# Coupling cycles spread over the turn, features a turn ahead, and attention scores moved into the head of the turn

## The reference

```
x = _layernorm(x + _L0_attn_ref(x, ...))     # random features: exp(x.w - |x|^2/2), times a matrix
x = _layernorm(x + _L0_xattn_ref(x, ctx...)) # 16-head attention over 120 keys
x = _layernorm(x + _L0_ffn_ref(x, ...))      # "coupling": 3 cycles of a 4-layer net and a twist
x = _layernorm(x + _L1_attn_ref(x, ...))     # Mamba-like: conv, silu, softplus, 16-state scan
x = _layernorm(x + _L1_xattn_ref(x, ctx...)) # gelu(x @ ctx.T) * (x @ ctx.T) @ ctx
x = _layernorm(x + _L1_ffn_ref(x, ...))      # router, best of 8 experts, times its gate
```

## Time and profile before

| | |
|---|---|
| median of 3 runs | 3458.91 us (3455.02 to 3460.43) |
| profiled execution, its own time | 3453.69 us |
| its span, first to last instruction | 3451.9 us |
| PE / DVE / ACT / POOL busy | 77% / 75% / 46% / 44% of the span |
| TensorE clock granted, mean | 0.805 of full speed |
| HBM traffic | 13 GB/s over the span |

### The profile page before, as it was taken

How to read it: one execution, slowest core, us unless ns; L and a number is a source line. 1 busy time by engine, 2 the same in 40 slices (tenths; PEclk the granted TensorE clock), 3 DMA queues, 4 the chain that set the end, 5 groups by cost and what they waited for, 6 DMA issues and landing times.

```text
span 3451.9 us, 41745 instructions
## 1 busy us (share of the span) xinstructions
PE 2672.9 (77%) x10956; PEld 1520.7 (44%) x10956; DVE 2598.4 (75%) x4316; ACT 1571.6 (46%) x2870; POOL 1505.1 (44%) x1159
## 2 busy tenths in 40 slices
PE   5877878787787878878787787887778787787746
PEld 3435435354453535445354453544445354443413
DVE  2387786968779696877868778687887968778693
ACT  1363545535455443544545444443544544454440
POOL 0064461725427172561725427163461726436180
PEclk8868778887887888788887887878878887888777
DMA  3000000000000000000000000000000000000000
GB/s 116 8 8 0 21 1 28 0 22 6 0 28 0 27 0 21 7 0 27 0 22 6 0 28 0 27 0 7 21 0 27 0 22 6 0 12 0 12 0 12
DMA packets 16786, 45.63 MB, mean 13 GB/s; under 512 B 2376, under 2 KB 6992, under 8 KB 16336
## 3 DMA queue, kind: packets, MB, share of 16 engines
q1 hardware_dynamic: 16592, 43.90, 3.5%
HBM read 35.50 MB, written 8.39 MB: 13 GB/s over the span
## 4 chain that ended last, share of the span: by engine, by line
PE 48%; DVE 25%; issue 12%; ACT 9%; POOL 3%; DVEq 1%; ACTq 0%; DMA 0%; SPq 0%; POOLq 0%
PE bank L487 46%; DVE h_ring L1014 9%; POOL ysum L1534 3%; DVE x L392 3%; DVE x L1111 2%; DVE smax L919 2%; ACT a_ring L1379 2%; PE bank L400 2%; DVE ln_stats L374 2%; DVE xpad L1020 1%; ACT bank L1374 1%; ACT spare L1319 1%; DVE qT L969 1%; DVE x L1091 1%; DVE x12T L971 1%
## 5 line engine op out<-in xcount | busy, mean ns | idle before, releaser
L1534 POOL TENSOR_TENSOR ysum<-ysum,h_ring 128x512 f32<-128x512 f32 x896 | 1152.3, 1286 | 490.8 <-DVE h_ring L1014 428.1
L1014 DVE TENSOR_TENSOR_SCAN h_ring<-a_ring,bank 128x512 f32<-128x512 f32 x1024 | 1170.6, 1198 | 103.8 <-ACT a_ring L1379 51.3
L487 PE MATMUL bank<-w_expert_w,x45T 128*128 128x512 f32 x1024 | 621.5, 746 | 197.8 <-DVE x L1111 196.2
L1379 ACT ACTIVATE a_ring<-soft,decay 128x510 f32<-128x510 f32 x1024 | 660.2, 712 | 119.7 <-DVE h_ring L1014 118.2
L487 PEld LDWEIGHTS bank<-w_expert_w,x45T 128*128 128x128 f32 x1024 | 221.7, 235 | 485.1 <-DVE x L1111 247.7
L1515 POOL TENSOR_TENSOR x<-x,w_rows 128x1024 f32<-128x1024 f32 x16 | 47.9, 2992 | 851.7 <-PE bank L400 851.7
L1289 ACT ACTIVATE spare<-bank 120x512 f32<-120x512 f32 x256 | 138.1, 591 | 449.5 <-PE bank L487 449.5
L487 PE MATMUL bank<-spare,w_cn_w 128*128 128x256 f32 (+2 forms) x768 | 278.4, 472 | 44.0 <-ACT spare L1323 20.3
L400 PE MATMUL bank<-w_ident,x 128*128 128x128 f32 x640 | 135.7, 347 | 223.4 <-DVE x L392 223.4
L1111 DVE SCALAR_TENSOR_TENSOR x<-bank,weight,x 128x256 f32<-128x256 f32 x512 | 212.3, 471 | 72.2 <-PE bank L487 72.2
L966 DVE TENSOR_SCALAR couple<-gate,gate_scale,base 128x256 f32<-128x256 f32 x96 | 40.0, 416 | 275.9 <-ACT gate L1333 275.9
(11 more groups left out here) (144 smaller groups left out, 3836.5 us busy)
## 6 DMA issues: line engine op xcount, KB each, us to landing
x0T<-in_xT SPq DMA_DIRECT2D x16, 512.0 KB, 3.3
x<-in_x SPq DMA_DIRECT2D x16, 512.0 KB, 4.2
out<-x SPq DMA_DIRECT2D x16, 512.0 KB, 3.2
ctxT<-in_ctxT SPq DMA_DIRECT2D x16, 240.0 KB, 4.3
ctxTb<-in_ctxT SPq DMA_DIRECT2D x16, 240.0 KB, 2.6
ctxb<-in_ctx SPq DMA_DIRECT2D x16, 240.0 KB, 3.0
w_expert_w<-in_expert_w SPq DMA_DIRECT2D x1, 2048.0 KB
w_winT<-in_winT SPq DMA_DIRECT2D x1, 1024.0 KB
```

The costliest lines, as they stand in the source:

```text
L487: return pe.matmul(o, l, r, start=start, stop=stop)
L1014: scanned.then(v.tensor_tensor_scan(h_ring[:, k % HRING, :], a_ring[:, k % RING, :, :].rearrange("p b s -> p (b s)"), xc2, 0.0, ALU.mult, ...
L1379: a.activation(a_ring[:, k % RING, :, 1:S], delta[:, c, :].rearrange("p (b s) -> p b s", b=NB)[:, :, 1:S], ACT.Exp, scale=decay[:, k:k + 1 ...
L1534: p.tensor_tensor(out=total, in0=first, in1=h_ring[:, k % HRING, :], op=ALU.add)\
```

## The change

Three groups' work is still done in each turn, but a fourth, nxt = f+1, is served in part:

- **Coupling.** The six steps are three cycles of two (`cycle(f, 0)`, `cycle(f, NB)`, `cycle(f, 2 * NB)`), apart from each other by decays on ACT, experts on PE and scans on DVE. Each has its own load of the GELU table and of the log/exp table behind it: 9 loads in a turn and not 5. The matmuls `mamba_out` no longer stand between the layers; they open the next turn, with the layernorm of that group behind them.
- **Features ahead.** The random features, keys, values, first projection and first layernorm of nxt are done in the second half of the turn, so x, xT and ctxT are loaded apart and earlier.
- **Scores into the head.** All 16 score steps and their maxima stand ahead of the first scan, between the parts of `mamba_in` and `convolve`, on three banks and not four.
- RING is 12 (8 before); softplus goes chunk by chunk; the squares of chunks 1 to 3 are made at decays 20, 34 and 48 (before: at the fifth decay of the chunk, 20, 36 and 52); a copy of m's x is kept for its layernorm (`keep`, 1024 elements on ACT).
- The loop has 13 turns; turn 15 stands behind it without an nxt.

The diff, cut to its core. In the three `turn` functions the guards (`if f is not None:` and the like) are left out, and what they guard keeps its indent; lines that were removed there are not shown.

```diff
-RING = 8
+RING = 12
 HRING = 6
 OUT_AFTER = 4
-SQUARE_AT = 4
+SQUARE_AT = (0, 20, 34, 48)
...
-        SCORES = [bank[0], bank[1], bank[2], bank[5]]
-        OUT12 = [bank[2], bank[0]]
+        OUT1 = [bank[2], bank[4]]
+        OUT2 = [bank[2], bank[0]]
+        QUERY = [bank[2], bank[0]]
+        TURN1 = [bank[0], bank[1]]
+        IN = [bank[4 + j % 2][:, :] for j in range(2 * IC)]
...
-                    if u >= 4:
-                        pe.wait_ge(smax_ready.sem, smax_ready.at(g, u - 2))
+                    if u >= 2:
+                        pe.wait_ge(smax_ready.sem, smax_ready.at(g, u - 1))
                     for e in range(DC):
                         for r in (r0, r0 + 1):
-                            last = mm(SCORES[r][:, e * 240:(e + 1) * 240],
+                            last = mm(bank[(u + r - r0) % 3][:, e * 240:(e + 1) * 240],
                                       qT[r * 32:(r + 1) * 32, e, t * P:(t + 1) * P],
...
+            def cycle(f, s):
+                for n in range(1, 5):
+                    for k in (s, s + 1):
+                        if n > 1 or s >= NB:
+                            layer(f, n, k)
+                        if n == 2 and k == 0:
+                            glob(f, 3)
+            def turn(f, m, b, nxt):
                     rotate_back(m, 1)
+                    mamba_out(b, 0, 12)
+                    norm_turn(pe, n1, f, TURN1)
+                    norm_turn(pe, n3, m, TURN)
+                    mamba_out(b, 12, 16)
+                    queries(f)
+                    mamba_in(m, 0, 2)
+                    scores(f, 0, 2)
+                    mamba_in(m, 2, IC)
                     norm_turn(pe, n4, b, MB)
+                    scores(f, 2, 4)
                     gated_in(b)
+                    mamba_in(m, IC, IC + 2)
+                    scores(f, 4, 6)
+                    mamba_in(m, IC + 2, 2 * IC)
+                    scores(f, 6, 8)
+                    turn_maxima(f, m)
+                    gated_out(b)
+                for k in range(SLOTS + 2):
                         attend(f, k, k + 1)
+                        if k == 3:
+                            norm_turn(pe, n5, b, MB)
+                        elif k == 5:
+                            router(b)
+                        elif k == 9:
+                            turn_weights(b)
+                        elif k == 11:
+                            expert_bias(b)
+                        elif k in (13, 15):
+                            experts(b, (k - 13) // 2, (k - 11) // 2)
+                    rfs(nxt, 0, f)
+                    experts(b, 2, 3)
+                    project(f, n2, ctxnT_ready, ctxnT, wo, DC, OUT2)
+                    rfs(nxt, 1, f)
+                    experts(b, 3, 4)
                     norm_turn(pe, n2, f, TURN)
+                    experts(b, 4, 5)
                     layer(f, 1, 0)
                     glob(f, 1)
+                        pe.wait_ge(feats_ready.sem, feats_ready.at(nxt, DC))
                     layer(f, 1, 1)
                     glob(f, 2)
+                    cycle(f, 0)
+                    keys(nxt, f)
+                    values(nxt, f)
+                    experts(b, 5, 9)
+                    cycle(f, NB)
+                    experts(b, 9, 12)
+                    first_project(nxt)
+                    experts(b, 12, 16)
+                    cycle(f, 2 * NB)
                     rotate_back(f, 0)
...
+            def convolve(g, c0):
+                if c0 == 0:
+                    conv_chain.start(v, g)
...
+            def turn_(f, m, b, nxt):
+                    ln4_sum(b)
+                    norm_apply(v, n4, b)
+                    convolve(m, 0)
+                    maxima(f, 0, 2)
+                    convolve(m, 2)
+                    maxima(f, 2, 8)
+                    negate_maxima(f)
                     gated(b)
+                    copy_maxima(f)
+                states(m, 2)
                     ln5_sum(b)
+                states(m, 3)
                     norm_apply(v, n5, b)
+                states(m, 6)
                     route(b)
+                states(m, 7)
                     pick_expert(b)
+                states(m, 8)
+                    normalize_context(f, 0)
                     start_sum(b)
+                states(m, 12)
                     combine(b, 0, 2)
+                states(m, 16)
+                    normalize_context(f, 1)
+                states(m, 18)
+                    ln2_sum(f)
+                states(m, 19)
+                    norm_apply(v, n2, f)
                     combine(b, 2, 4)
+                states(m, 23)
+                    global_base(f)
+                states(m, 28)
+                    rotate(f, 0)
+                    rotate(f, 1)
+                states(m, 33)
                     combine(b, 4, 6)
+                    values(nxt)
+                states(m, 37)
                     combine(b, 6, 8)
+                states(m, 44)
+                    rotate(f, 2)
+                    rotate(f, 3)
+                states(m, 50)
                     combine(b, 8, 10)
+                states(m, 52)
                     combine(b, 10, 12)
+                states(m, 54)
+                    ln1_sum(nxt)
                     combine(b, 12, 14)
+                states(m, 60)
                     combine(b, 14, 16)
+                    ln6_stats(b)
+                    rotate(f, 4)
+                    rotate(f, 5)
+                states(m, len(PLAN))
                     ln3_sum(f)
+                    norm_apply(v, n1, nxt)
                     norm_apply(v, n3, f)
...
+            def softplus(g, c0, c1):
+                for c in range(c0, c1):
+                    a.wait_ge(xc_ready.sem, xc_ready.at(g, c + 1))
+                    a.activation(soft[:, c, :], xc[:, c, :], ACT.Exp, scale=-1.0).then_inc(exp_ready.sem, 1)
+                for c in range(c0, c1):
+                    a.wait_ge(exp_ready.sem, exp_ready.at(g, c + 1))
+                    a.activation(soft[:, c, :], soft[:, c, :], ACT.Ln, bias=1.0).then_inc(soft_ready.sem, 1)
-                    if n == (SQUARE_AT if c else 0):
-                        if c:
-                            a.wait_ge(scanned.sem, scanned.at(g, AFTER["scan", c - 1, STATES - 1]))
-                        a.activation(xc2, xc[:, c, :], ACT.Square).then_inc(xc2_ready.sem, 1)
+                    if k in SQUARE_AT:
+                        c2 = SQUARE_AT.index(k)
+                        if c2:
+                            a.wait_ge(scanned.sem, scanned.at(g, AFTER["scan", c2 - 1, STATES - 1]))
...
+            def cycle(f, s):
+                gelu()
+                for n in range(1, 5):
+                    for k in (s, s + 1):
+                        network(f, n, k)
+                        if n < 3 and s == 0:
+                            if n == 1 or k == 0:
+                                global_network(f, n + k if n == 1 else 3)
+            def turn_(f, m, b, nxt):
+                    norm_copy(a, n1, f, TURN1)
                     norm_copy(a, n3, m, TURN)
                     queries(f)
+                    mamba_in(m, 0, 2)
+                    norm_rstd(a, n4, b)
+                    mamba_in(m, 2, IC)
+                    norm_copy(a, n4, b, MB)
+                    silu()
+                    silu_conv(m, 0, IC)
+                    mamba_in(m, IC, 2 * IC)
+                    gated(b)
+                nat()
+                    softplus(m, 0, 1)
+                decays(m, 3)
                     norm_rstd(a, n5, b)
+                    softplus(m, 1, IC)
+                decays(m, 8)
+                    softmax(f, 0, 2)
+                decays(m, 10)
+                    softmax(f, 2, 4)
                     norm_copy(a, n5, b, MB)
+                decays(m, 12)
+                    softmax(f, 4, 6)
+                    softmax(f, 6, 8)
                     route(b)
+                decays(m, 16)
+                    softmax(f, 8, 10)
+                    invert_sums(f, 0)
                     copy_weights(b)
+                decays(m, 18)
+                    softmax(f, 10, 12)
+                    softmax(f, 12, 14)
+                decays(m, 20)
+                    softmax(f, 14, 16)
                     invert_sums(f, 1)
+                decays(m, 24)
+                    feat(nxt, 0)
+                decays(m, 26)
+                    keep(m, b)
+                    feat(nxt, 1)
+                decays(m, 28)
                     norm_rstd(a, n2, f)
+                decays(m, 30)
                     copy_and_sum(f)
+                decays(m, 34)
+                    cycle(f, 0)
+                    nat()
+                    keys(nxt)
+                decays(m, 48)
+                    cycle(f, NB)
+                    nat()
                 decays(m, STEPS)
+                    cycle(f, 2 * NB)
                     nat()
+                    norm_rstd(a, n1, nxt)
+                    norm_rstd(a, n3, f)
```

(12 more changed lines are left out.)

521 lines of the change are left out of this document (226 added, 295 removed).

## The result

The changed kernel takes 3780.36 us (median of 4 runs, 3778.14 to 3780.74) beside 3458.89 us for the kernel before. The ratio is 1.0933 (95% interval 1.0916 to 1.0951). The prediction was 3643 us with a range of 3390 to 3765: slower, as forecast, but by 321 us and not by 184. Its profiled execution has a span of 3778.3 us.

The account below looks back on a forecast made before the run. DVE's fixed-order work plus its waits bound the turn: 165 + 53 = 218 us against 205.7, +172 over 14 turns, +15 for part turns, giving 3643 us after small corrections; range 3390 to 3765.

Parts of the forecast that it names:

- The gate waits: DVE's waits for the coupling gates, 17.2 us a turn before, would fall to near 2 with the cycles spread.
- Rivals 1, 2 and 4: PE keeps its clock, lower part 3466 to 3520 us (0.13); faster, 3345 to 3405 (0.17); equal trade, within 0.2% (0.05).
- Rival 3: POOL's adds slow six rotates by 24 us a turn, 20 beyond those counted: 3920 us; chance 0.05.
- the high end of each wait: Each DVE wait priced with PE at half clock for 4 to 8 us behind its long waits; sum 60 us.
- The maxima: In the head, DVE waits for scores queued on PE behind mamba_in and gated_in: 7.7 to 9.0 us.
- The base: DVE wants the global base right behind scan 21, with nothing covering its chain from decay 33: 5.1 us.
- The last "out": At the turn's end DVE waits for POOL's last add and product, no longer covered by the first rotate: 2.7 us.
- The second and third gates: Behind the base, the gates of the second cycle come 1.0 to 1.2 us late.
- The experts behind the base: Experts 10 and 11, between the base and the turn's end, come 0.5 to 2.4 us late.
- Expert 1, the second projection and the second rstd: Between the first scan and the base, DVE waits 4.3 to 5.0 us for these.
- The router: Behind six scans, DVE waits for the router's logits, whose chain runs through softmax and attention: 7.4 to 10.3 us.
- The part turns: Turns 1 and 16 have half the waits; the last has mamba_out and the fourth layernorm in front: +15 us (0 to +40).

Follow-up runs that it names:

- e9: Changed kernel with the three coupling cycles together again at the turn's end, behind all decays, experts and scans but the last "out"; 3826.2 us.
- e16: e11 with the base and first cycle behind 31 instead of 28 scans and the second cycle behind 46 instead of 44; 3577.8 us.
- e6: Changed kernel with POOL's additions of states 2 to 15 on 8 of 512 columns, leaving out most of the sum; 3840.7 us.
- e14: e13 with more scans ahead of the first normalization, the first and second experts, n2's sum, the base and the first two cycles; 3556.8 us.
- e8: Changed kernel with 28 matmuls without use on PE where it waits, ahead of two maxima waits and the first softmax; 3698.1 us.
- e11: e10 with the first normalization behind 12 instead of 8 scans, first experts behind 14, and n4's rstd ahead of two mamba_in copies; 3508.8 us.
- e10: e5 with 21 matmuls without use a turn on PE, ahead of score pairs, turned maxima, n5's turning and the router; 3682.2 us.
- e5: Changed kernel with four edits: mamba_in ahead of scores, router two softmax pairs earlier, base behind five more scans, last seven scans ahead of third-cycle rotates; 3618.6 us.
- e1: Changed kernel with all of mamba_in ahead of the scores on PE, and both convolution halves ahead of the maxima on DVE; 3764.1 us.
- e2: Changed kernel with the fifth layernorm's turning and the router two softmax pairs earlier on PE and ACT; 3769.3 us.
- e12: e6 with the 28 matmuls without use of e8; 3762.7 us.
- e18: Changed kernel with one reduction without use on DVE between a turn's last "out" and the third layernorm; 3779.6 us.
- e19: Changed kernel with three reductions without use on DVE between a turn's last "out" and the third layernorm; 3777.4 us.
- e15: e14 with the matmuls without use of e10; 3576.3 us.
- e13: e11 without its matmuls without use; 3592.8 us.

## Why the prediction was right, and where its size was wrong

**Direction and mechanism: right.** The turn is DVE's work plus its waits. The gate waits went to 3.9 us a turn ("near 2" was forecast), and each wait that the prediction named is there. e9 shows the gain side apart from the loss side: 3.4 against 23.0 us a turn. The first scan came 55.7 us behind time 0, inside the forecast 47.6 to 56.6, but by more waits and less work than forecast. Rivals 1, 2 and 4 fell with the time: the turn is longer than each allows.

**DVE's work: 165 forecast, 152.8 measured.** That is 12 us a turn in the kernel's favour. The frame took DVE's work as fixed, and it isn't: the same 269 instructions took 152.8 us here and 162.2 in e16. Rival 3 (POOL slows the rotates, 24 us a turn) fell for the changed kernel: e6 shows that POOL's additions cost it 2.1 us a turn. Its mechanism is real and smaller, 8.6 us a turn at the most (e14, e16). Of the 10 us that DVE's work fell from before, 3.5 are the fifth layernorm's apply (1.35 us, and 4.81 before). That POOL stood beside it, and beside other small steps for the rest, I only argue.

**The waits: 53 forecast (46 to 60), 72.5 of idle time measured, 69 of it in waits of half a microsecond or more.** This is the step that failed: the high end of each wait. By stretches the waits are 29.8 us up to the first scan (forecast 18.9 to 27), 27.5 from there to the base (23.3 to 26.9) and 11.8 from the base on (4.2 to 6.3). By its terms:
- The maxima: 7.7 to 9.0 forecast, 16.0 measured. The two score pairs behind long waits were slow, and so were two of the three `mamba_in` rows between the scores. e8 gives the size: with a clock of 1.00 in the head the maxima wait 11.1 us, and all waits up to the first scan are 20.5, inside the forecast. So 4.9 of the missing us are the clock. Another part is the price of four score matmuls, 0.8 in the forecast and 1.08 at the whole clock.
- The base: 5.1 forecast, 6.2 measured. PE's part is longer (1.48 us of wait for its layer against 0.68 in the earlier trace rows), not the table's. That is the clock again: the layer's four matmul records take 2.03 us, in e8 they take 1.13, and e8's base waits 5.15 us, as forecast.
- The last "out": 2.7 forecast, 4.2 measured. POOL does the last seven additions in 9.31 us, where seven scans take 7.88, and starts 1.4 us behind them; I had it one addition behind.
- The second and third gates: 1.0 to 1.2 forecast for the second cycle, 2.3 and 1.6 measured.
- The experts behind the base: 0.5 to 2.4 forecast, 3.7 measured (1.04, 1.34 and 1.35). Expert 1, the second projection and the second rstd: 4.3 to 5.0 forecast, 5.6 measured.
- The router: 7.4 to 10.3 forecast, 9.5 measured. The waits for `mamba_out`, for the fourth rstd, the convolution's second half, the first scan and the fourth decay lay within their forecasts or 0.3 us from them.

The rows behind the base and the last "out": ACT's timeline of the kernel after, from decay 33 to the base, as in the earlier trace rows, and POOL's at the turn's end, as in the earlier trace rows:

```profile
2080.53 0.72 ACT L1440 ACTIVATE a_ring<-soft,decay 128x510 f32<-128x510 f32 x1 [1.28 <-DVE h_ring L1057]
2081.27 1.28 ACT L1459 ACT_TABLE_LOAD   x1
2082.56 0.84 ACT L1370 ACTIVATE spare<-bank,w_columns 128x256 f32<-128x256 f32 x2
...
2085.88 0.47 ACT L1374 ACTIVATE spare<-bank,w_columns 128x256 f32<-128x256 f32 x1 [1.48 <-PE bank L522]
2086.40 0.26 ACT L1361 ACTIVATE gt<-bank,half_gb 128x2 f32<-128x2 f32 x1
```

```profile
2165.08 9.31 POOL L1625 TENSOR_TENSOR ysum<-ysum,h_ring 128x512 f32<-128x512 f32 x7 [8.17 <-DVE h_ring L1057]
2174.47 1.26 POOL L1628 TENSOR_TENSOR ysum<-ysum,res 128x512 f32<-128x512 f32 x1
```

The table's load again takes 1.28 us with the next activation 1.29 behind its start. The drain of 1380 ns that the Trainium skill (ScalarE: Activation LUTs, What ACT_TABLE_LOAD costs) counts beside it isn't there, and leaving it out of the sum was right.

**The bound itself.** The high end of each wait took PE at half clock "for 4 to 8 us behind each of its long waits". The runs show slow stretches of 16 us (e11), 25 (e10), 45 (e6) and 50 (e5, at a mean of 0.53), in e10 and e11 with PE busy nearly throughout. The forecast's high end was 60.2 us a turn, and 69 were measured. e8 shows that the clock is most of that in the head (it gave 9.3 us back, and nothing over the forecast was left). Behind the base, where 11.8 us stand against 6.3, no run separates the clock from the order.

**The part turns: +15 forecast (0 to +40), +52 measured.** The first store comes 38 us later than a turn's growth of 19.6 explains, and the end takes 15 more. I had halved the waits of turn 1; DVE waits 75 us in it, as long as in a full turn, with the next group's features besides.

**Two errors that partly cancel** (work 12.2 too high, waits 19.5 too low) left 7.3 us a turn, 102 us over 14 turns. The part turns gave the other 37. (The forecast's own sum is 3 us short: 3641 and the 5 that the profiled execution lay below the median make 3646.)

**What stays open.** Six kernels of different content share a mean turn of 225.3 us (after, e1, e2, e12, e18, e19) and three one of 215.0 (e5, e15, e16). The kernel before, too, goes between two lengths within one execution. Windows of the kernel before, a turn of each:

```profile
755.05:959.85 204.80, 162.50 (x685) 92.92 (x685) 162.74 (x268) 97.56 (x179) 93.68 (x72) 0.83 0.03 12
1577.70:1785.90 208.20, 166.91 (x685) 94.67 (x684) 162.81 (x268) 97.56 (x179) 93.64 (x72) 0.80 0.03 12
```

The work is the same and the granted clock is not. The steady turns of all kernels here lie at 204.8, 208.2, 211.6, 215.0, 218.5, 221.9, 225.3, 228.7 and 232.1 us, or have such a length as the mean of two: some 3.4 us apart. (e13, with three lengths in turn, is the exception.) So a gain of a few us in one turn can show as nothing or as a whole step, and the small gains above don't give the size of a wait. That a loop's turn and PE's clock settle on each other would explain both this and the odd gains of single edits. It is argued from the lengths and was not isolated.

## What to carry to other kernels

Where one engine works in a fixed order, price every wait twice: with the other engine at its full clock and with it slow for the whole stretch up to the next long dense piece, not for a few microseconds. When a single edit takes a wait away and the time stays, look in the same turn for the wait that took its place, and try two or three edits together before calling the chain something else. Before spreading a chain of dependent steps over a turn, ask what covered it: here the scans had covered the base, and spreading was worth 3.4 us a turn where its waits had counted 17.2. When scans are moved to cover a wait, look at what then stands beside POOL's additions: the rotates took up to 8.6 us a turn more.

## What the runs showed of the hardware that I had not expected

- PE's granted clock stays at its lower level (0.50, 1.2 GHz) for 25 us with PE busy 24.60 of them, mostly in matmuls of 32 and 120 rows, and fell to it after 18 us in which PE was busy throughout (e10).
- 28 more matmuls without use made a kernel 82 us faster (e8), and 21 made others 64, 20 and 28 us slower and one 84 us faster.
- The same instructions in the same kernel took 217.8 and 232.8 us in alternate turns (e1).
- Taking 60 us a turn of work off POOL made the kernel 60 us slower (e6: POOL busy 33.5 us a turn against 93.1).
- A product of 128x256 on DVE takes 426 ns on average without full additions on POOL (e6) and 1013 ns with the rotates among them (e16).
